# A token-shift subtraction of an RWKV-style mixing stage goes from VectorE to GpSimd

## The reference, cut to what matters

```python
x = x + _L0_attn_a_ref(_layernorm(x), ...)   # causal windowed attention
x = x + _L0_ffn_ref(_layernorm(x), ...)      # slot feed-forward
x = x + _L0_attn_b_ref(_layernorm(x), ...)   # this stage
x = x + _L0_ffn_ref(_layernorm(x), ...)      # slot feed-forward again

def _L0_attn_b_ref(x, maa_x, ...):           # x: (B, T, C), already normed
    xx = jnp.concatenate([jnp.zeros_like(x[:, :1]), x[:, :-1]], axis=1) - x
    xxx = x + xx * maa_x
    lora = jnp.tanh(xxx @ maa_w1).reshape(B, T, 5, D_MIX)
    m = jnp.einsum('btfd,fdc->fbtc', lora, maa_w2)
    xw = x + xx * (maa_w + m[0])             # and xk, xv, xr, xg likewise
    r = xr @ Wr; k = xk @ Wk; v = xv @ Wv
    ...
    return yn * g @ Wo
```

## Time and profile before

| What | us |
|---|---|
| Median of 2 timed runs of the kernel before | 6707.93 (6704.15 to 6711.71) |
| The profiled execution | 6695.99 |
| Its span on the slowest core (core 7), first to last instruction | 6694.4 |
| The fastest core of the same execution (core 2) | 6655.5 |
| Busy in the span: TensorE / VectorE / ScalarE / GpSimd | 2566.3 / 2185.3 / 1959.2 / 83.1 |

### The profile page before, as it was taken

One profiled execution on the slowest core, in us unless ns is written; L12 is line 12 of the kernel. 1 busy time (PEld: TensorE's weight loads), 2 busy tenths in 40 slices (PEclk: granted clock), 3 DMA queues, 4 the chain that ended last, 5 costly groups with the idle time before them and its releaser, 6 DMA issues.

```text
span 6694.4 us, 43251 instructions; the slowest of 8 cores (6655.5 to 6694.4 us)
## 1 busy us (share of the span) xinstructions
PE 2566.3 (38%) x13290; PEld 1162.5 (17%) x13290; DVE 2185.3 (33%) x4504; ACT 1959.2 (29%) x3022; POOL 83.1 (1%) x120
## 2 busy tenths in 40 slices
PE   2555555645233222343525343443525343233221
PEld 1222222222111110121211211121211211111110
DVE  1212212121122212354444545354444535122222
ACT  2454454646044300122131313122131313034300
POOL 0000000000000000000000000000000000000000
PEclk9666656565655555655656575655657565666555
DMA  4000000010411144400000000000000000311145
GB/s 77 13 26 26 26 26 26 1 51 1 83 38 38 24 91 176 88 1 25 0 26 0 0 26 0 25 1 25 0 26 0 0 26 0 82 38 38 38 83 182
DMA packets 87423, 242.88 MB, mean 36 GB/s; under 512 B 7837, under 2 KB 17181, under 8 KB 87072
## 3 DMA queue, kind: packets, MB, share of 16 engines
q0 software_dynamic: 59936, 135.04, 8.6%
q1 hardware_dynamic: 27264, 105.06, 4.7%
HBM read 235.03 MB, written 67.11 MB: 45 GB/s over the span
## 4 chain that ended last, share of the span: by engine, by line
PE 31%; DVE 25%; ACT 23%; DMA 11%; issue 7%; another core or an unknown queue 1%; DVEq 1%; POOL 0%; ACTq 0%; POOLq 0%; PEld 0%; PEldq 0%; SPq 0%
PE psC L1744 4%; ACT Wslot L585 4%; ACT L585 4%; DVE b_ubuf L1694 3%; ACT hfeat L331 2%; ACT hfeat L326 2%; DVE b_mixb L1702 2%; PE psC L2207 2%; PE psC L656 2%; PE psC L1770 2%; ACT hfeat L397 2%; PE psT L386 2%; DMA xin<-x 2%; DMA x2d<-xout 2%; PE psA L942 1%
## 5 line engine op out<-in xcount | busy, mean ns | idle before, releaser
L386 PE MATMUL psT<-identb_s,htok 128*128 128x128 bf16 x832 | 96.9, 309 | 915.7 <-DVEq L367 825.8
L326 ACT ACT_TABLE_LOAD x34 | 43.6, 1283 | 1156.3 <-DMA xin<-x 505.6
L585 ACT ACT_TABLE_LOAD x192 | 246.3, 1283 | 268.1 <-PE psC L571 268.1
L1934 PE MATMUL psT<-identb_s,b_xx 128*128 128x128 bf16 x256 | 32.4, 306 | 736.5 <-DVE b_xx L1922 736.5
L1744 PE MATMUL psC<-b_mixb,Wslot 128*128 128x512 bf16 x1024 | 259.4, 421 | 43.6 <-DVE b_mixb L1702 43.6
L599 DVE TENSOR_TENSOR Wslot<-Wslot,maskA_s 128x512 bf16<-128x512 bf16 x128 | 54.4, 425 | 611.8 <-ACT Wslot L585 611.8
L1800 ACT ACT_TABLE_LOAD x8 | 10.3, 1283 | 812.1 <-PE psD L1791 812.1
L386 PEld LDWEIGHTS psT<-identb_s,htok 128*128 128x128 bf16 x832 | 84.6, 143 | 932.8 <-issue 932.8
L571 PE MATMUL psA<-Qf,Kf 64*128 64x512 bf16 x192 | 108.6, 566 | 264.2 <-ACT Wslot L585 256.3
L338 DVE TENSOR_SCALAR stats<-stats 128x4 f32<-128x4 f32 x34 | 5.8, 170 | 607.9 <-ACT hfeat L331 607.9
L585 ACT ACTIVATE Wslot<-psC,cvals_s 128x256 bf16<-128x256 f32 (+2 forms) x384 | 174.8, 514 | 0.0
(11 more groups left out here) (378 smaller groups left out, 6185.6 us busy)
## 6 DMA issues: line engine op xcount, KB each, us to landing
xin<-x1d SPq DMA_DIRECT2D x32, 2048.0 KB, 9.8
x1d<-xout POOLq DMA_DIRECT2D x16, 2048.0 KB, 13.4
xin<-x SPq DMA_DIRECT2D x10, 2048.0 KB, 11.2
x2d<-xout POOLq DMA_DIRECT2D x8, 2048.0 KB, 13.6
xin<-x2d SPq DMA_DIRECT2D x8, 2048.0 KB, 11.1
out<-xout POOLq DMA_DIRECT2D x8, 2048.0 KB, 13.8
Wslot<-fWhhT POOLq DMA_DIRECT2D x6, 2048.0 KB, 16.0
Wslot<-fWihT POOLq DMA_DIRECT2D x6, 2048.0 KB, 15.6
```

The costliest lines, as they stand in the source:

```text
L326: ctx.inc(sc.activation(scr[:, tt * 1024:(tt + 1) * 1024], xin[:, tt, :], AF.Square, accum_out=stats[:, 8 + tt:9 + tt]), "AC")
L386: ctx.inc(t.transpose(psT[:, bank + dc * 128:bank + (dc + 1) * 128], hb[:, tt, dc * 128:(dc + 1) * 128], identb[:]), "PE")
L585: ctx.inc(sc.activation(Ph[:, kt * 512 + qo:(kt + 1) * 512], ps[:, 0:512 - qo], AF.Exp, bias=cvals[:, 1:2], scale=0.125), "AC")
```

## The change

The three instructions of `f_xx` are issued on GpSimd instead of VectorE, with the same operands, and count on the semaphore `GP`. GpSimd waits for ScalarE's last copy into `hfeat`, for TensorE's end of the block before, and for VectorE's count. A `gpsync` follows them. VectorE's first instruction of `f_xxx` waits for that count, and so does ScalarE before it uses `hfeat` as scratch in the next block (`hfeat_gp`).

```diff
             if g.get("hfeat_dv") is not None:
                 sc.wait_ge(ctx.sem["DV"], g["hfeat_dv"])
+            if g.get("hfeat_gp") is not None:
+                sc.wait_ge(ctx.sem["GP"], g["hfeat_gp"])
             scr = hfeat[:].rearrange("p a b -> p (a b)")
...
                 "hfeat_dv": bprev.get("hfeat_dv"),
+                "hfeat_gp": bprev.get("hfeat_gp"),
                 "psT_ac": bprev.get("psT_ac"),
...
-            def f_xx(v, ha=ctx.hfeat_ac, bpe=bprev.get("blk_pe")):
-                v.wait_ge(ctx.sem["AC"], ha)
+            def f_xx(gp, ha=ctx.hfeat_ac, bpe=bprev.get("blk_pe")):
+                gp.wait_ge(ctx.sem["AC"], ha)
                 if bpe is not None:
-                    v.wait_ge(ctx.sem["PE"], bpe)
-                ctx.inc(v.tensor_tensor(xx[:, :, 0:1], prevc[:].unsqueeze(2),
-                                        hfeat[:, :, 0:1], ALU.subtract), "DV")
-                ctx.inc(v.tensor_tensor(xx[:, :, 1:512], hfeat[:, :, 0:511],
-                                        hfeat[:, :, 1:512], ALU.subtract), "DV")
-                ctx.wait(v, "DV")
-                ctx.inc(v.tensor_copy(prevc[:].unsqueeze(2), hfeat[:, :, 511:512]),
-                        "DV")
-            ctx.on("vector", f_xx)
-
-            def f_xxx(v):
+                    gp.wait_ge(ctx.sem["PE"], bpe)
+                ctx.wait(gp, "DV")
+                ctx.inc(gp.tensor_tensor(xx[:, :, 0:1], prevc[:].unsqueeze(2),
+                                         hfeat[:, :, 0:1], ALU.subtract), "GP")
+                ctx.inc(gp.tensor_tensor(xx[:, :, 1:512], hfeat[:, :, 0:511],
+                                         hfeat[:, :, 1:512], ALU.subtract), "GP")
+                ctx.wait(gp, "GP")
+                ctx.inc(gp.tensor_copy(prevc[:].unsqueeze(2),
+                                       hfeat[:, :, 511:512]), "GP")
+            ctx.on("gpsimd", f_xx)
+
+            gp_xx = ctx.gpsync()
+            bprev["hfeat_gp"] = gp_xx
+
+            def f_xxx(v, gp_xx=gp_xx):
                 ctx.wait(v, "LDW")
+                v.wait_ge(ctx.sem["GP"], gp_xx)
                 for oc in range(NDC):
                     ctx.inc(v.scalar_tensor_tensor(
```

## The result

The kernel before had a median of 6698.51 us (16 runs beside this one), the changed kernel 6727.58 us (17 runs). The ratio is 1.0043, 95% interval 1.0033 to 1.0053: slower by 0.43% or 29 us, and inside the 2% that the prediction called "same". The sign and the place were as forecast. The size was not: 29 us against 51.5.

The account below looks back on a forecast made before the run. Engines that wait for one another were taken to bound the kernel. Seven blocks each swap 2.60 us on VectorE for 9.95 us on GpSimd, 51.5 us on a base of 6707.9: 6759 us, range 6722 to 6808.

Parts of the forecast that it names:

- same: Whole kernel: a change below about 2% (134 us), which a measurement cannot tell from no change; chance 0.93.
- The subtraction lies on the chain in seven blocks: Blocks two to eight: a longer subtraction lengthens each block fully; the first block hides it behind the last weight DMA.
- The large subtraction, 9.0 us: 4088 elements a partition on GpSimd: 9.0 us a block, 2.2 ns an element, between 4.1 and 12.8 us.
- The prediction's own sign of a mis-sized rate: GpSimd's row for the large subtraction below 5 or above 13 us would show its rate was mis-sized.
- The small things, 0.95 us: On GpSimd each block: two instructions on 8 elements, 0.3 us each, and 0.35 us for waits and handover.
- TensorE's longer pause, nothing: Before L1635 the pause grows from 11.9 to about 19 us, adding nothing; at worst 3.9 us a block.
- The sum: Per block 9.95 - 2.60 = 7.35 us, times seven 51.5 us, giving 6759 us, +0.77%.
- A start-up in every block: GpSimd's subtraction: about 6 us more a block to begin computing, 93 us in all, 6801 us; chance 0.13.
- Almost free: GpSimd streams both operands together, subtraction 2.3 to 4.9 us, 3 to 20 us in all, 6711 to 6728; chance 0.10.
- Slower by over 2%: GpSimd handles bf16 element by element, 5.1 ns or more each; at 6 ns 160 us, 6868 us; chance 0.05.

Follow-up runs that it names:

- Two doses on two engines: About five or twelve us a block more than the kernel before, from GpSimd's subtraction or from repeats on VectorE; ratios 1.0048 and 1.0135 on GpSimd, 1.0065 and 1.0133 on VectorE.
- the split: Kernel before with the large subtraction divided, six channel groups on VectorE and two on GpSimd; 6721.1 us, ratio 1.0012.
- the dose of twelve us on GpSimd: Changed kernel with the large subtraction done twice on GpSimd; 6787.59 us, ratio 1.0135.
- the larger doses: Large subtraction done six times on VectorE in the kernel before, 6785.65 us, or twice on GpSimd in the changed kernel, 6787.59 us.
- five us on VectorE: Kernel before with the large subtraction done three times on VectorE and once more for one channel group; 6739.84 us, ratio 1.0065.
- all three kernels that tried it: Subtraction divided between both engines, 6721.1 us; only the small instructions on GpSimd, 6697.24; changed kernel with an extra fp32 GpSimd subtraction beside VectorE's mix, 6757.39.

## Why the prediction was right or wrong

- *The subtraction lies on the chain in seven blocks.* Right. Two doses on two engines moved the ruler alike, and the first block's wait still ended with the DMA.
- *The large subtraction, 9.0 us.* This is the step that failed, by its size: it takes 6.99 us. The choice between 4.1 and 12.8 us had doubled two rates to 2.2 ns an element. One of them, VectorE's 1.20 ns, is already that of an instruction with two inputs (L2127, a multiplication), so nothing called for doubling it. That 2.2 is GpSimd's rate for fp32 (2.19 ns) is a coincidence; for bf16 it is 1.71. 7 x 2.0 = 14 of the 51.5 us. The prediction's own sign of a mis-sized rate, a row below 5 or above 13 us, was too wide to show it.
- *The small things, 0.95 us.* Measured, with 0.16 us for VectorE's old start behind ScalarE, 7.89 - 0.16 - 6.99 = 0.74 us with the hops, so 1.5 us less in seven blocks. Together the gap grew by 5.13 and not 7.35 us a block, 36 us in all.
- *TensorE's longer pause, nothing.* Wrong, by 4 to 6 us in the other direction: the upper clock came later in the second eight matmuls. The prediction had named 3.9 us a block as the worst; it was about 0.7. That the longer pause is the cause is not shown. The loss does not grow with it: the split, with 13.4 us of pause, lost 6.9 us in seven blocks, and the dose of twelve us on GpSimd, with 24.1, lost 4.7. With 26 unused matmuls in the pause, the last of them 10.5 us before the real ones, the second eight still took 488 ns, while the kernel before has 388 behind 11.9 us of idleness.
- *The sum.* By the ruler the stage grew by 40 us, 11.5 less than the forecast. The median of the slowest core grew by 29 and, measured again, by 0.48% or 32 us. In that second measurement the mean span of all eight cores grew by 37 us (6676 to 6713, over 11 and 5 runs) and that of the slowest core by 30 (6697 to 6728). So what is missing lies in how far the slowest core stands above the mean, 21 us before and 14 after. Why that shrank stays open; at the larger doses it was 20. In the profiled executions the part behind the last tanh of the ruler, mostly the second feed-forward, was 6 us shorter in the mean of the eight cores with the changed kernel (1276 to 1270 us), and 6 us longer with five us on VectorE (1282), though no edit adds or removes work there beyond the last block. So the 40 us of the stage are shown, and the missing 8 to 11 of the time are not explained. The forecast time, 6759 us, also stood on a base of two runs (6707.93) that lies 9.4 us above the median of sixteen.
- *The rivals.* A start-up in every block: not there, all eight instructions are alike within 2 ns. Nor is there one in the first block, where the small subtraction starts 0.20 us after ScalarE's end. Almost free: no, the gap grew by 5.13 us and not by 0.5 to 2.9. (With the prediction's own 0.95 us for the small things that range should have been 0.65 to 3.25 us, 5 to 23 in all.) Slower by over 2%: no, 1.71 ns an element and not 5.1.

## What to carry to other kernels

Ask first whether the engine that gives work away has anything else to do meanwhile. Here the next instruction needed the result, so the move only exchanged a fast instruction for one three times as long. Where there is other work, check its operands: a VectorE instruction with two inputs in SBUF and a GpSimd instruction that reads SBUF ran one after the other in all three kernels that tried it. What pays in a serial stretch is to begin on the part of the input that is already there.

## What the runs showed of the hardware that was not expected

- GpSimd's two-input subtraction depends on the type: 1.71 ns an element in bf16, 2.19 in fp32.
- A GpSimd instruction on 8 elements a partition lasts 2.27 us instead of 0.22 when a VectorE subtraction is under way, and a VectorE mix instruction 4.98 us instead of 0.74 when it meets a GpSimd subtraction. The Trainium skill says so (SBUF — State Buffer, "SBUF: two separate sides"): whichever comes first has the shared ports for its whole instruction. All three kernels agree.
- TensorE's clock was granted at 1.00 after a few unused matmuls, and at 0.52 again for work that came after 5.0 us of idleness; behind 0.87 us of idleness the real matmuls ran at the upper level from the first.
